# A Fourier-operator tower on one core: forward transforms of both images in one pass, and another order of units

## What is computed

```python
h = einsum('bhwi,ic->bhwc', x, fc0_w) + fc0_b            # 3 -> 64 channels, then channels first
for l in range(4):
    xf = rfft2(h)                                         # 2-D transform, 16+16 by 16 modes are kept
    top = einsum('bixy,ioxy->boxy', xf[:, :, :16, :16], w1[l])
    bot = einsum('bixy,ioxy->boxy', xf[:, :, -16:, :16], w2[l])
    sc = irfft2(the kept modes in place, the rest zero)
    y = sc + einsum('bihw,oi->bohw', h, pw_w[l]) + pw_b[l]
    h = gelu(batch_norm(y))
```

## Time and profile before

| | |
|---|---|
| median of 3 runs | 4752.23 us (4751.26 to 4759.73) |
| the profiled execution | 4746.3 us, of which its span is 4744.5 us |
| PE busy (matmul) | 3513.1 us, 74% |
| VectorE (DVE) busy | 2431.2 us, 51% |
| ScalarE (ACT) busy | 2252.6 us, 47% |
| granted TensorE clock, mean | 0.868 |
| the three fuse phases | about 295 to 1168, 1363 to 2209 and 2407 to 3241 us of the span |

### The profile page before, as it was taken

One profiled execution on the slowest core, in us unless ns is written; L12 is line 12 of the kernel. 1 busy time (PEld: TensorE's weight loads), 2 busy tenths in 40 slices (PEclk: granted clock), 3 DMA queues, 4 the chain that ended last, 5 costly groups with the idle time before them and its releaser, 6 DMA issues. The chain is left out here.

```text
span 4744.5 us, 143699 instructions
## 1 busy us (share of the span) xinstructions
PE 3513.1 (74%) x65092; PEld 2052.3 (43%) x65092; DVE 2431.2 (51%) x2474; ACT 2252.6 (47%) x2644; POOL 173.3 (4%) x249
## 2 busy tenths in 40 slices
PE   6768878886756777775757777775599999468877
PEld 4634444443633444443634444444444444353432
DVE  4644444443555666654656666664533333364556
ACT  3634444453644545444635555454466666222322
POOL 2022000000000000000000000000000101100000
PEclk8879988898878888888878889888799999669778
DMA  8756454546767667666767677768734332003043
GB/s 301 278 140 172 126 129 112 130 108 215 268 181 212 194 205 217 201 199 224 248 197 216 196 212 221 206 187 286 263 133 158 139 145 89 11 1 64 10 86 68
DMA packets 162317, 800.22 MB, mean 169 GB/s; under 512 B 26889, under 2 KB 33361, under 8 KB 111854
## 3 DMA queue, kind: packets, MB, share of 16 engines
q1 hardware_dynamic: 150876, 776.16, 54.2%
q0 software_dynamic: 7936, 13.65, 0.9%
q10 hardware_dynamic: 2898, 1.17, 0.1%
HBM read 448.68 MB, written 342.23 MB: 167 GB/s over the span
## 5 line engine op out<-in xcount | busy, mean ns | idle before, releaser
L822 PE MATMUL bank<-fb,arena 64*64 64x128 f32 x16384 | 699.0, 310 | 342.7 <-issue 236.1
L822 PEld LDWEIGHTS bank<-fb,arena 64*64 64x64 f32 x16384 | 613.2, 199 | 640.0 <-issue 584.3
L1034 ACT ACTIVATE arena<-bank 128x1024 f32<-128x1024 f32 x384 | 393.0, 1023 | 888.9 <-PE bank L954 546.3
L839 DVE TENSOR_TENSOR arena<-bank,arena 128x1024 f32<-128x1024 f32 x384 | 466.2, 1214 | 523.8 <-PE bank L822 523.2
L1079 DVE STREAM_TRANSPOSE arena<-arena 128x1024 f32<-128x1024 f32 x384 | 470.3, 1225 | 210.4 <-ACT arena L1024 203.3
L954 PE MATMUL bank<-arena,wst 64*64 64x512 f32 x3072 | 471.8, 672 | 36.3 <-issue 27.2
L831 DVE STREAM_TRANSPOSE arena<-bank 128x1024 f32<-128x1024 f32 x256 | 317.2, 1239 | 271.3 <-PE bank L812 271.3
L970 PE MATMUL bank<-arena,fwq 32*32 32x256 f32 x12288 | 329.6, 403 | 145.7 <-issue 141.4
L1027 ACT ACTIVATE arena<-arena,shift,scale 128x1024 f32<-128x1024 f32 x256 | 316.3, 1235 | 240.5 <-DVE arena L839 240.5
L1086 DVE STREAM_TRANSPOSE arena<-bank 128x1024 f32<-128x1024 f32 x192 | 237.6, 1237 | 375.5 <-PE bank L970 375.5
L1041 ACT ACTIVATE arena<-arena 128x1024 f32<-128x1024 f32 x384 | 402.4, 1048 | 0.7
(11 more groups left out here) (238 smaller groups left out, 3740.3 us busy)
## 6 DMA issues: line engine op xcount, KB each, us to landing
y_dram<-arena SPq DMA_DIRECT2D x192, 1024.0 KB, 11.1
arena<-y_dram SPq DMA_DIRECT2D x96, 2048.0 KB
arena<-spec_in SPq DMA_DIRECT2D x32, 2048.0 KB, 8.8
spec_out<-arena SPq DMA_DIRECT2D x128, 512.0 KB, 8.2
arena<-in_w_modes SPq DMA_DIRECT2D x28, 2048.0 KB, 14.0
arena<-spec_out SPq DMA_DIRECT2D x112, 512.0 KB, 15.1
spec_in<-arena SPq DMA_DIRECT2D x24, 2048.0 KB, 8.6
spec_in<-arena SPq DMA_DIRECT2D x4, 4096.0 KB, 13.7
```

The lines of the kernel that those rows point to most:

```text
L822: mm = pe.matmul(hpx(bank[2 * s + i][CHAN[v], :])[:, :, j * S:(j + 1) * S], a2[p % 2][CHAN[i], :, v, 4 * T + j], hpx(fb2[CHAN[i], :]), sta ...
L839: dve.tensor_tensor(chunk(p, T), slot(s), chunk(p, T), ALU.add).then_inc(y_added, 1)
L1034: act.activation(chunk(p, T), slot(NEXT_SLOT[T]), ACT.Copy).then_inc(evicted, 1)
```

## The change

In `w_dft` both images go through in one call of 512 columns, where there were two of 256. `h_dft` makes 64 output columns with one weight tile (real and imaginary part together, tiles of 32x64), where it made 32 (32x32); this changes the order of the partitions of `xs`, so that `store_spectra` needs four transfers of 32 partitions for the one of 128. The third `y` unit moves from slot 1 to slot 0, and the order of the units on TensorE, ScalarE and VectorE is another one, with the waits that belong to it. The stores of a pair are four transfers of 512 KB, and the first phase's stores of spectra are two for each one, with contiguous pieces of 2 KB where there were 4 KB. The DRAM tensors `spec_out`, `y_dram` and `w_modes` get another shape over the same order of bytes; `w_even` (1 MB a layer) is laid out in blocks of 2 KB rows.

```diff
@@ sync_spectrum0
-                gs = slice(t * MB // GI, (t + 1) * MB // GI)
-                sp.dma_start(spec_in[:, :, gs].rearrange("h p g x -> p h (g x)"), spec0[t % 3]).then_inc(spec0_stored[min(t, 1)], 16)
+                for g in range(MB // GI):
+                    sp.dma_start(spec_in[:, :, t * MB // GI + g].rearrange("h p x -> p h x"),
+                                 spec0[t % 3][:, :, g * GI * MC:(g + 1) * GI * MC]).then_inc(spec0_stored[min(t, 1)], 16)
...
@@ load_pair, slots
-            sp.dma_start(pb[p % NS], y_dram[p].rearrange("p (i x) -> p i x", i=2)).then_inc(p_loaded[p % NS], 16)
+            sp.dma_start(pb[p % NS].rearrange("p i (t x) -> p (i t) x", x=BK), y_dram[p].rearrange("p t x -> p t x")).then_inc(p_loaded[p % NS], 16)
-        Y_SLOT = (0, 1, 1, 0)
+        Y_SLOT = (0, 1, 0, 0)
@@ store of sync_fuse
                 for i in range(2):
-                    sp.dma_start(y_dram[p].rearrange("(v c) (i x) -> i c v x", v=2, i=2)[i], pb[p % NS][CHAN[i]]).then_inc(p_stored[p % NS], 16)
+                    for v in range(2):
+                        sp.dma_start(y_dram[p, CHAN[v], 4 * i:4 * i + 4].rearrange("c t x -> c t x"),
+                                     pb[p % NS][CHAN[i], v].rearrange("c (t x) -> c t x", x=BK)).then_inc(p_stored[p % NS], 16)
@@ store_spectra
-                sp.dma_start(spec_in[:, :, g].rearrange("h p x -> p h x"), xs.rearrange("p h m k b -> p h (m k b)")).then_inc(spec_stored, 16)
+                for v in range(2):
+                    for ro in range(2):
+                        to, at_ = ro * C + v * HB, v * C + ro * HB
+                        sp.dma_start(spec_in[:, to:to + HB, g].rearrange("h p x -> p h x"),
+                                     xs[at_:at_ + HB].rearrange("p h m k b -> p h (m k b)")).then_inc(spec_stored, 16)
@@ tensor_fuse
             def rows_of(p, hc):
-                if p > 0:
-                    pe.wait_ge(drained, (l * NP + p) * 4 - 3 + 2 * hc)
-                    pe.sem_inc(waited[pe.engine], 1)
+                n = l * NP + p
+                if hc == 0 and p > 0:
+                    pe.wait_ge(drained, n * 4 - 3)
+                if hc == 1 and p == 1:
+                    pe.wait_ge(drained, n * 4 - 2)
+                if hc == 1 and p > 1:
+                    pe.wait_ge(evicted, n * 4 - 4)
+                pe.sem_inc(waited[pe.engine], 1)
                 rows(pe, l, p, hc, ROWS_SLOT[hc])
...
-            def w_dft(p, i):
+            def w_dft(p):
...
-                            mm = pe.matmul(bank[4 + g][QUAD[c], 0:256], fwq[QUAD[g], s * 32:(s + 1) * 32],
-                                           hT[p % 2][QUAD[g], i, :, s, c * CQ:(c + 1) * CQ],
+                            mm = pe.matmul(bank[4 + g][QUAD[c], :], fwq[QUAD[g], s * 32:(s + 1) * 32],
+                                           hT[p % 2][QUAD[g], :, :, s, c * CQ:(c + 1) * CQ].rearrange("p i h c -> p (i h) c"),
                                            start=(s == 0), stop=(s == 1), tile_position=(32 * g, 32 * c))
...
-                    for j in range(4):
-                        ro, v = j // 2, j % 2
-                        col = (k * 2 + ro) * K1
+                    for v in range(2):
                         for c in range(4):
-                            mm = pe.matmul(bank[4 + c][QUAD[j], 256:512], ghq[QUAD[c], col:col + K1],
+                            mm = pe.matmul(bank[4 + c][CHAN[v], 256:512], ghq[QUAD[c], k * 2 * K1:(k + 1) * 2 * K1],
                                            t1[p % 2][QUAD[c], hh * 2 + v, :, :, ri * M2:(ri + 1) * M2],
-                                           start=(k == 0), stop=(k == 3), tile_position=(32 * c, 32 * j))
+                                           start=(k == 0), stop=(k == 3), tile_position=(32 * c, C * v))
...
             for n in range(NP + 2):
                 now, before, after = n < NP, 0 < n <= NP, n + 1 < NP
+                if before:
+                    next_of(n - 1, 2)
                 if now:
                     y_of(n, 0)
                     y_of(n, 1)
+                if after:
+                    rows_of(n + 1, 0)
                 if n > 1:
                     h_dft(n - 2)
                 if before:
                     next_of(n - 1, 3)
-                if after:
-                    rows_of(n + 1, 0)
                 if now:
                     y_of(n, 2)
+                if after:
+                    rows_of(n + 1, 1)
                 if before:
-                    w_dft(n - 1, 0)
+                    w_dft(n - 1)
                 if now:
                     next_of(n, 0)
-                if after:
-                    rows_of(n + 1, 1)
-                if now:
+                    next_of(n, 1)
                     y_of(n, 3)
-                    next_of(n, 1)
-                if before:
-                    w_dft(n - 1, 1)
-                if now:
-                    next_of(n, 2)
```

More of the change, by code:

```diff
@@ L99, in tower_layout @@
     out["w_turned"] = np.ascontiguousarray(out["w_modes"][:, 0][:, :, turned])
+    out["w_modes"] = np.ascontiguousarray(out["w_modes"].reshape(L, NCH, P, MC * C // BK, BK))
     out["pw_t"] = np.ascontiguousarray(pw_w.transpose(0, 2, 1))
@@ L527, in store @@
                     row = t % 2 * C + t // 2 * HB
-                    sp.dma_start(spec_out[c, row:row + HB], m_sb[c % 2][t * HB:(t + 1) * HB]).then_inc(mixed_stored[c % 2], 16)
+                    sp.dma_start(spec_out[c, row:row + HB].rearrange("p g x -> p g x"),
+                                 m_sb[c % 2][t * HB:(t + 1) * HB].rearrange("p g v x -> p g (v x)")).then_inc(mixed_stored[c % 2], 16)
             def ahead():
@@ L782, in load_group @@
             sp.dma_start(grp[g % 2].rearrange("p (c v) b o -> p c (v b o)", v=2)[:, cs],
-                         spec_out[cs, :, g].rearrange("c p v x -> p c (v x)")).then_inc(grp_loaded[g % 2], 16)
+                         spec_out[cs, :, g].rearrange("c p x -> p c x")).then_inc(grp_loaded[g % 2], 16)
         GRP_LOADS = [(NG // 2 - 1) * Q + 2, NG // 2 * Q]
@@ L846, in sync_fuse @@
             if first:
-                sp.sem_inc(spec_stored, 16)
+                sp.sem_inc(spec_stored, 64)
             def store(p):
@@ L938, in next_of @@
                 pe.wait_ge(h_made, n * 4 + T + 1)
-                if T < 2:
+                if T == 0:
+                    pe.wait_ge(drained, n * 4 + 3)
+                if T == 1:
                     if p < NP - 1:
-                        pe.wait_ge(rows_turned, n * 2 + 3 + T)
-                    elif T == 1:
-                        pe.wait_ge(drained, n * 4 + 3)
+                        pe.wait_ge(rows_turned, n * 2 + 4)
+                    else:
+                        pe.wait_ge(evicted, n * 4)
                 if T == 2:
@@ L1046, in scalar_fuse @@
                 if before:
+                    evict(n - 1, 0)
                     evict(n - 1, 1)
+                    square(n - 1, 0)
                     evict(n - 1, 2)
                     gelu(n - 1, 3)
-                    square(n - 1, 0)
+                    square(n - 1, 1)
                 if now:
                     gelu(n, 0)
-                if before:
-                    square(n - 1, 1)
-                if now:
                     gelu(n, 1)
@@ L1061, in scalar_fuse @@
                     gelu(n, 2)
-                    evict(n, 0)
                 if before:
@@ L1107, in vector_fuse @@
                     add(n, 1)
+                if after:
+                    turn_rows(dve, l, n + 1, 0, ROWS_SLOT[0])
+                if now:
                     px_turn(n, 0)
@@ L1110, in vector_fuse @@
                     h_turn(n - 2)
-                if after:
-                    turn_rows(dve, l, n + 1, 0, ROWS_SLOT[0])
                 if now:
                     add(n, 2)
-                    px_turn(n, 1)
-                if before:
-                    w_turn(n - 1, 0)
                 if after:
@@ L1120, in vector_fuse @@
                 if now:
+                    px_turn(n, 1)
                     px_turn(n, 2)
+                if before:
+                    w_turn(n - 1, 0)
+                if now:
                     add(n, 3)
```

56 lines of the change are left out of this document (27 added, 29 removed).

## The result

The changed kernel takes **4337.58 us** (median of 4 runs, 4332.76 to 4346.47), against 4751.74 for the kernel before: a ratio of 0.9132, 95% interval 0.9107 to 0.9156. The prediction was 4520, range 4425 to 4650. The direction was right, but the gain was 414 us where some 230 were forecast, and the time lies under the range.

A forecast was written before the change was run, and what follows sets the result against it. TensorE was taken to bound a clean period, with VectorE close behind. Terms of -156 (later fuse phases), -87 (first fuse phase) and +9 (small things) made -234 from 4746.3: 4512, as runs' median 4518, say 4520; range 4425 to 4650.

The forecast's parts named there:

- The transforms: TensorE's w_dft and h_dft units: -0.7 and -0.8 us a pair, bounds 0 and -1.5 together, work falling to 14.4 us.
- The order: Walk of the new unit order in a pair: clean period 16.1 us, giving back only part of the 1.5 us.
- The late transfer: Last spectra quarter, needed by the rows unit: TensorE stops 8 us every fourth pair in later fuse phases, 22.8 a pair.
- Rival 1: No late transfer of spectra in the later fuse phases: 20.8 us a pair, 4400 us; chance 0.2.
- so a period is 17.0 clean + 5.7 of missing instructions + 2.7 of slower clock: Breakdown of the old later-phase period of 25.4 us: TensorE's clean work, stops for instruction packets, and reduced clock.
- the stop before y(n,0): First fuse phase: a 2.37 us stop, waiting for gelu(n-1,3) behind evict(n-1,2), was to stay.
- SP issues more transfers, beside PE's work: Small term for SP's extra transfers: 0.4 to 0.6 us each, running beside TensorE's work.
- Instructions in the later phases: TensorE's stops for instruction packets: 2.55 packets a pair at 1.15 us, 2.9 us a pair, bounds 0.5 and 4.1.
- Rival 2: Neither transform gains: other periods 22.3 us, later phases 23.6 a pair, first fuse phase 25.0, 4610 us; chance 0.2.
- rival 3: Slower: every instruction fetch waits on busy DMA engines, 4.0 us a packet, period 28.1 us, 4840 us; chance 0.05.

The follow-up runs named there:

- e5: Changed kernel with two-pass w_dft, old h_dft tiles, two pair stores and one spectra store restored, leaving only the new order of units: 4733.3 us.
- e4: Changed kernel with each piece of the next group's spectra issued one pair earlier: 4217.5 us.
- e8: Kernel before, with the pieces of the group's spectra issued one iteration earlier: 4755.62 us, ratio 1.0013.
- e1: Changed kernel with w_dft in two passes of 256 columns again: 4469.82 us.
- e2: Changed kernel with h_dft in the old 32x32 tiles (128 MATMULs) and the spectra stored in one transfer again: 4491.42 us.
- e3: Changed kernel with the pair's stores in two transfers of 1 MB again: 4420.83 us.
- e6: Kernel before, with each pair stored in four transfers of 512 KB instead of two of 1 MB, same runs of 8 KB: 4605.7 us.
- e15: Kernel before, with each pair stored in eight transfers of 256 KB instead of two, runs of 8 KB: 4495.0 us.
- e7: Kernel before, with h_dft in 32x64 tiles and the spectra stored in four transfers: 4620.84 us.
- e17: Changed kernel with the spectra's piece one pair earlier, eight pair stores of 256 KB and the pair's load issued ahead of them: 4190.62 us.
- e9: Changed kernel with 32 more TensorE calls a pair, of 8 columns each, ahead of w_dft: 4485.95 us.
- e10: Changed kernel with 4 more TensorE calls a pair, of 512 columns each, ahead of w_dft: 4381.62 us.
- e12: Kernel before, with only the pair's 2 MB load split into four transfers, its two stores as they were: 4786.85 us.

## Why the prediction was wrong in size and right in direction

**The transforms** (15.9 to 14.4 us of TensorE's work): right. `w_dft` 2.28 for 2.15, `h_dft` 1.91 for 2.0, together 4.19 for 4.15. The Trainium skill, TensorEngine Tiling (Array Packing), "Available Configurations", counts tiles (16 of 32x32, 8 of 32x64), and by that count alone `h_dft` would not have got shorter. The trace does not agree with that use of the count, since the unit went from 2.84 to 1.91 us; by the rows, something other than the columns had set the 32x32 round.

**The order**: the walk gave a clean period of 16.1 and the trace has 16.24. In the first phase 20.6 were forecast; thirteen of the trace's 31 periods (by line 1104) are 20.1 or 20.2. That the order gives back little is what e5 shows, by way of -36, +10 and +22 us.

**The late transfer**: right, place and size. Fourteen stops, 142 us in all, 10 each where 8 were forecast; in the second fuse phase six four-pair loops take 532.5 us (1258.84 to 1791.32 by line 1104), 88.7 each, and in the third 90.9, for the 91.2 forecast. The 44.5 us of the sum held with 42.8, though its 2 us of start-up and 1.3 for the four stores stood on estimates and no run measured them singly. e4, with the piece issued earlier, and e8 show the cause. Rival 1 falls.

**The first step that failed: "so a period is 17.0 clean + 5.7 of missing instructions + 2.7 of slower clock", and what became of the last two in the first fuse phase.** Its 3.7 us beside the clean period were to become 2.9. The phase took 20.9 us a pair over the first 29, so by the forecast's clean period of 20.6 they became 0.3, and by the 20.1 of the trace 0.8. In 290 to 955 us TensorE waited for issue 76.6 us,

```profile
PE bank L828 <- issue: 73.4, 32, 2.4
...
PE bank L999 <- issue: 2.2, 2, 1.8
PE bank L973 <- issue: 1.0, 2, 0.5
```

and all but some 3 us of that is the stop before y(n,0), which was forecast to stay. Before, the same four lines had 81.3 + 31.6 + 16.6 + 6.0 = 135.5 in 860 us. With the other stops gone the clock stood at 0.97, where it had been 0.90. (3.7 - 0.3 - 0.8) x 30 = 78 us of the 88 missed in this phase. The experiments say which part did it. Undoing the two transforms costs 45 + 53 = 98 us here (e1, e2), 3.2 us a pair, where the sum gave them 1.5 as work and 0.8 for stops and clock; undoing the stores costs 37 (e3), 1.2 a pair, where it gave nothing; and the order is worth 1.2 (e5), for 0.6.

**The second: "SP issues more transfers, beside PE's work", that is, the four stores priced at nothing.** They are worth 83 us in the changed kernel and 142 in the one before (e3, e6), with shorter stops for issue in both. The prediction had the sign of a cost in view (between 0 and 4 us later for the piece) and did not ask what else stands behind a store. Had it taken e6's -142, the sum would have been 4378 us, still over the result, since part of the two failures is the same time.

**Instructions in the later phases**: 83 packets in 730 us (80 forecast for 31 pairs) and, with the small ones, 72.4 us of waits for issue: 2.3 us a pair for 2.9 forecast, 0.87 a packet for 1.15. The term was mis-sized, and e3 names what by: its two stores bring the waits from 66.8 back to 90.6 us in 1240 to 1840. The rule that I weighed, the Trainium skill, DMA: Bandwidth & Descriptors, "Queues, rings and completion order", would have made the stops near nothing as I used it, with a packet taken as short. The trace does not agree with that: they are 2.3 us a pair. The other reading that the prediction left open, that a whole transfer's share on a DMA engine counts as one packet, is not excluded, and stops that shrink with the stores (e6, e15) would fit it.

**The account**, on the span (its 25.5 us for the second phase without the short last period should have been 25.7; the mean of the two phases stays 25.4): forecast -87, -78, -78 and +9, measured -175, -120, -95 and -10. The misses are 88 in the first phase, 59 in the later two and 19 outside of them. In the later two the four-pair loops are as forecast, so the 59 lie in the ends, where no next group is waited for (7 loops with a stop, where 7.5 were counted, and five pairs without), and in the loops being 0.1 to 0.6 us a pair shorter; this I have only worked out. The 19 were not followed, and no run undid the first phase's new stores of spectra by themselves. Rival 2 falls (e7), rival 3 too: the waits for issue were 2.3 and 2.5 us a pair in the later phases, none over 5 us.

**Left open.** Why smaller stores shorten the stops. The runs exclude the load's delay and the mere count of transfers, not the slower arrival of the same bytes, and they do not say what a smaller load with its old runs would do. Whether a packet waits behind a store's share on its DMA engine isn't shown, as the trace has no request times. Why the load ahead of the stores gains 50 us before and loses 37 in e17 is open too.

## What to carry to other kernels

Where TensorE's idle time has the releaser "issue" and packets of the instruction queue land just before it goes on, count instructions a pair like work, and try the size of the stores first: four for two gave 142 us, eight some 250. Ask of a reordering which transfer had only its last microsecond of room (here 0.7 us), and move that issue in the same edit. Read a gain by phase: here the first one, where no piece comes late, gained the most, its granted clock going from 0.90 to 0.97; how much of the gain is the clock's was not measured.

## What the runs showed of the hardware that was not expected

- Sixty-four MATMULs of 8 columns with their weight loads, 0.5 us of TensorE's time, cost 1.5 us a pair (e9); eight of 512 columns, 0.96 us, cost 0.46 (e10).
- Stores of 1 MB, 512 KB and 256 KB with the same runs of 8 KB: 4747.9, 4605.7 (e6) and 4495.0 us (e15). A load of 2 MB in four parts, with runs of 4 KB for 16: 4786.9 (e12).
- The granted clock over the first fuse phase was 0.97 after and 0.90 before, with TensorE busy for 85% and 80% of the stretch; in the later phases 0.89 and 0.87, at 71% and 73%.
- In the kernel after, SP's issue of four stores took 3.1 us in one iteration (1320.53) and 9.3 us in another, behind the spectra's stores (1307.01).
